# A graph network of four blocks on one core: the matrix that moves sums from rank to node order holds one over each node's count in place of one

## What is computed

```python
count = max(seg(ones), 1)                       # edges that end in a node, at least one
# block 0 (layer k = 0)
h = relu(h @ W_self.T + (seg(h[src]) / count) @ W_neigh.T + bias)
# block 1 (layer k = 1): product over edges of h[src] * edge_attr * filter(edge_weight), then softplus(agg @ W3 + b3)
# block 2 (layers k = 2, 3, 4), relu after the first two
h = (seg(h[src]) / count) @ W_agg[i] + h @ W_root[i] + b[i]
# block 3 (layers k = 5, 6, 7): attention with self loops, leaky relu, batch norm
h = leaky_relu(seg(ex * (h @ W)[src]) / denom + self_term + bias)
```

## Time and profile before

| | before |
|---|---|
| median of 3 runs | 8981.9 us (8965.29 to 8985.5) |
| profiled execution, its own time | 8979.64 us |
| profiled execution, span on the core | 8977.9 us |
| instructions | 96878 |
| busy: POOL, DVE, PE, ACT | 6350.5, 5163.1, 4441.1, 1376.7 us |
| TensorE clock granted, mean | 0.638 |

### The profile page before, as it was taken

The page is one execution under the profiler, slowest core; times in us unless marked ns, Lnnn a source line. Parts: engine busy times, 40 slices in busy tenths (PEclk is TensorE's granted clock), DMA queues, the critical chain, the costliest instruction groups (busy, mean ns, idle before and its releaser), DMA issues.

```text
span 8977.9 us, 96878 instructions
## 1 busy us (share of the span) xinstructions
PE 4441.1 (49%) x25313; PEld 3544.6 (39%) x25313; DVE 5163.1 (58%) x15662; ACT 1376.7 (15%) x2233; POOL 6350.5 (71%) x6609
## 2 busy tenths in 40 slices
PE   4655566665433344333533348354276452673532
PEld 3444433333433344333433345254253442543532
DVE  6786577776433343333433348686378773596844
ACT  6666634333100000000100010000010000100000
POOL 5777477776677767777677757777767777677774
PEclk7777777776655566565665555576555665656755
DMA  6555467775221121112211212332123331223311
GB/s 177 156 155 157 135 193 203 200 198 149 69 52 52 52 59 52 53 52 53 59 52 52 52 54 77 112 117 73 38 69 112 118 88 41 71 89 111 112 52 31
DMA packets 598961, 852.69 MB, mean 95 GB/s; under 512 B 130268, under 2 KB 404941, under 8 KB 597456
## 3 DMA queue, kind: packets, MB, share of 16 engines
q0 software_dynamic: 211168, 413.92, 17.8%
q1 hardware_dynamic: 372748, 381.31, 13.9%
q10 hardware_dynamic: 14688, 53.48, 1.5%
HBM read 652.71 MB, written 195.51 MB: 94 GB/s over the span
## 4 chain that ended last, share of the span: by engine, by line
POOL 69%; issue 24%; DVE 3%; PE 2%; DMA 1%; ACT 0%; POOLq 0%; ACTq 0%; DVEq 0%
POOL rows L821 41%; POOL rows L851 24%; POOL nd L834 2%; POOL at_first L827 2%; DMA rows<-table,src_t 1%; PE PS L1161 0%; POOL acc L868 0%; DVE H L1859 0%; DVE H L1858 0%; DVE H L2014 0%; DVE H L2013 0%; DVE H L2012 0%; DVE moments L1597 0%; PE PS L1169 0%; PE PS L1133 0%
## 5 line engine op out<-in xcount | busy, mean ns | idle before, releaser
L821 POOL DMA_INDIRECT rows<-table,src_t x3910 | 3724.7, 953 | 1491.2 <-issue 1263.9
L1667 DVE TENSOR_TENSOR acc<-acc,PS 128x128 f32 x5474 | 1552.7, 284 | 2956.5 <-PE PS L1244 1729.4
L851 POOL DMA_INDIRECT rows<-table,src_t x2346 | 2283.1, 973 | 923.2 <-issue 750.1
L1244 PE MATMUL PS<-onehot,rows 128*128 128x128 f32 x6256 | 1413.1, 417 | 2241.1 <-DMA rows<-table,src_t 2241.1
L1244 PEld LDWEIGHTS PS<-onehot,rows 128*128 128x128 f32 x6256 | 1305.5, 318 | 2404.4 <-DMA rows<-table,src_t 2403.6
L1280 PE MATMUL PS<-onehot,rows 128*128 128x128 f32 x3060 | 678.9, 411 | 1196.5 <-DMA rows<-table,src_t 1134.0
L1280 PEld LDWEIGHTS PS<-onehot,rows 128*128 128x128 f32 x3060 | 627.7, 313 | 1241.5 <-DMA rows<-table,src_t 1183.8
L1751 DVE TENSOR_SCALAR onehot<-PS,loc_t,shared 128x128 f32<-128x128 f32 x2346 | 940.4, 402 | 0.5
L924 ACT ACTIVATE rows<-acc 128x128 f32 x343 | 77.9, 297 | 2641.8 <-DVE acc L1667 2638.2
L1353 PEld LDWEIGHTS PS<-als_bf,onehot 128*128 128x128 bf16 x7056 | 308.3, 119 | 427.3 <-DVE onehot L1934 269.6
L1643 DVE TENSOR_TENSOR onehot<-PS,loc_t 128x1024 f32<-128x1024 f32 x392 | 476.7, 1217 | 0.2
(11 more groups left out here) (320 smaller groups left out, 5744.0 us busy)
## 6 DMA issues: line engine op xcount, KB each, us to landing
rows<-table,src_t POOLq DMA_INDIRECT x6256, 2.9
staged<-rows ACTq DMA_DIRECT2D x102, 512.0 KB
H<-staged SPq DMA_DIRECT2D x102, 512.0 KB
soft_rows<-shared SPq DMA_DIRECT2D x196, 256.0 KB
H<-soft_rows SPq DMA_DIRECT2D x98, 512.0 KB, 3.9
prod_rows<-onehot SPq DMA_DIRECT2D x98, 512.0 KB, 5.0
shared<-in_edge_weight SPq DMA_DIRECT2D x195, 256.0 KB, 3.5
G<-in_edge_attr SPq DMA_DIRECT2D x97, 512.0 KB, 6.2
```

Of the source, the lines that this page charges most:

```text
L821: pool.indirect_dma_start(rows[:, h * HT + j, :], None, table[k % 2], at(src_t[:, t:t + 1]))\
L851: pool.indirect_dma_start(rows[:, g % 2 * HT + j, :], None, table[k % 2], at(src_t[:, t:t + 1]))\
L1244: last = mm(window_at(k, c, j), rows[:, r, :], onehot[:, r, :], start=True, stop=True)
L1667: tt(at, at, window_at(k, c, j), ALU.add).then_inc(added[h], 1 if j < n - 1 else HT - n + 1)
```

## The change

The matrix holds `1 / count` of the node where it held a one. For that `make_perms` gets a second scalar and a second operation. In `mean_layer` the multiplication by `rcount` is gone, and the addition of `T` reads PSUM and gives the signal `nodes_used`. The attention layers use the same matrix but want no division by the count, so `self_weights` multiplies `rden_n` by the count once in each of them. For that `count` itself is now kept at one or more.

```diff
-                step(ts(rcount[:], count[:], 1.0, None, ALU.max))
-                step(recip(rcount[:], rcount[:]))
+                step(ts(count[:], count[:], 1.0, None, ALU.max))
+                step(recip(rcount[:], count[:]))
 
             def make_perms(m):
                 wait(v, perm_turned, m)
                 for j in range(min(PERM_BLOCKS, NT - m * PERM_BLOCKS)):
                     b = m * PERM_BLOCKS + j
-                    last = ts(perm_in[:, j * D:(j + 1) * D], iota_ps, plocal[:, b:b + 1], None, ALU.is_equal)
+                    last = ts(perm_in[:, j * D:(j + 1) * D], iota_ps, plocal[:, b:b + 1], rcount[:, b:b + 1],
+                              ALU.is_equal, ALU.mult)
                 last.then_inc(perm_made, 1)
...
                     v.wait_ge(nodes_ready, turn[k] * NCH + c + 1)
-                    step(tt(g, as_tiles(by_node(c)), per_node(rcount, c), ALU.mult), nodes_used)
-                    step(tt(g, g, t, ALU.add))
+                    step(tt(g, as_tiles(by_node(c)), t, ALU.add), nodes_used)
...
                 step(recip(rden_n, rden_n))
                 step(tt(exs_n, exs_n, rden_n, ALU.mult))
+                step(tt(rden_n, rden_n, count[:], ALU.mult))
                 step(tt(T3, T3, exs_n.unsqueeze(2).broadcast_to([P, NT, D]), ALU.mult))
```

## The result

The changed kernel takes 8950.3 us (median of 10 runs, 8935.3 to 8965.9). The kernel before, run beside it, takes 8968.7 us (median of 10, 8965.3 to 8985.5). The ratio is 0.9976 with a 95% interval of 0.9967 to 0.9985: about 21.5 us (0.24%) less, in an interval of 13.5 to 29.6 us. Forecast were 16.3 us less, 8965.6 us, and a result just within 0.2%. The time is inside the range of 8948 to 8982, but the gain is five microseconds larger than forecast and lies just beyond 0.2%. The two times themselves must not be compared: the forecast was counted from 8981.9 us, the median of three runs, and ten runs of the kernel before give 13.2 us less than that. Nor do the times alone exclude a gain of 16.3 us, which lies in their interval; the stretches of the profiles do.

What follows compares the result with a forecast made beforehand. It took POOL's gathers to set the pace within passes, with DVE mattering only where POOL waits. 3.1 + 3.1 + 5.4 + 5.4 - 0.7 = 16.3 us off the median 8981.9 gave 8965.6 us, range 8948 to 8982.

Steps and rivals of the forecast that it cites:

- Where the gain comes from: Removing the instruction pays only in four stretches, after the passes of layers 0, 2, 3 and 4, where POOL waits.
- Layers 2 and 3, 3.1 us each: After these layers' passes PE becomes the bound in place of DVE, so each stretch gains 3.1 us of 9.0 removed.
- Layers 0 and 4, 5.4 us each: After these layers' passes the removed multiplication stands eight times on the chain, so each stretch gains 5.4 us.
- both rings: Layer 4's two interleaved cycles through DVE, ACT and PE, two chunks per turn: each turn falls from 10.30 to 9.58 us.
- The clock rival: PE's clock rises in layer 4, about 9 us more, again if layer 0 follows: 8957 or 8948 us; chance 0.14.
- the sign of being wrong: Wrong if any stretch's granted clock changes level, L1859 takes other than 0.69 us, or the edge passes change length.
- The wait that moves in the rings: In layers 0 and 4 ACT or PE replaces DVE, so only stretch ends gain: 9.1 us, time 8973; chance 0.10.
- Slower, by PE at the lower clock in layers 2 and 3,: PE falls to its lower clock there, 27 us more per layer, time 9027 us; chance 0.05.
- The attention layers, -0.7 us: The new multiplication in self_weights delays the two large instructions and POOL by 0.24 us per layer, 0.7 us lost in three.
- the bound on the other side: In the attention layers one more gather might slip ahead of DVE's large instruction, gaining up to 1 us per layer.
- The matrix, nothing: L1745 takes 402 instead of 342 ns, 49 times, 2.9 us of DVE time hidden under waits for ACT: nothing lost.

Runs made afterwards that it cites:

- gat_late: The changed kernel with the attention layers' multiplication by count moved behind the two large instructions on T; ratio 0.9988 to the kernel before.
- after_again: The changed kernel run again without any edit, on another chip than the first; ratio 0.9986 to the kernel before.
- the busy pair: The two kernels before_busy and after_busy, both with idle PE matmuls in layers 0 and 4; ratios 0.9992 and 0.9984 to the kernel before.
- before_again: The kernel before run again without any edit, on another chip than the first; ratio 1.0001 to the kernel before.
- costs_only: The changed kernel with a multiplication by ones put back in all four mean layers, leaving only the added work; ratio 1.0004 to the kernel before.
- before_busy: The kernel before plus six unused PE matmuls after each chunk's block of L1169 in layers 0 and 4; ratio 0.9992 to the kernel before.
- after_busy: The changed kernel plus six unused PE matmuls after each chunk's block of L1169 in layers 0 and 4; ratio 0.9984 to the kernel before.
- after_order: The changed kernel with ACT copying the windows of chunk c + 2 right after the product of chunk c; ratio 0.9971 to the kernel before.

## Why the prediction was right, and where it was wrong

**Where the gain comes from** held. The four stretches in which POOL waits for the table are where the time went; the executions with and without the instruction differ there by 8.4, 2.3, 2.5 and 8.1 us (layers 0, 2, 3, 4; means over the table's rows up to gat_late, without the two busy ones, of 67.6 and 59.2, 30.3 and 28.0, 30.7 and 28.2, 67.5 and 59.5). That is 21.3 us, against a gain of 21.5 us by the times on the first chip, and 15.6 us with an interval of 5.6 to 25.6 in after_again.

**Layers 2 and 3, 3.1 us each:** the mechanism held to 0.01 us. DVE waits for PE at each chunk, the chunks come every 1.786 us, and DVE's part is 3.1 us shorter. The term was a little too large, 2.3 to 2.5 us measured, since I took the gain at DVE's last relu for that at the first gather. In the profiles of the first chip that last piece takes 2.22 us (3286.17 to 3288.39), 0.3 us more than before. That the stores come closer together now is my reading; no run tested it.

**Layers 0 and 4, 5.4 us each:** this is the step that failed. The prediction wrote "So both rings go to 10.30 - 0.72 = 9.58 us". The count of instructions in it was right within 0.7 us, as the busy pair shows. What failed was that PE's part of the turn, 3.89 us, was carried over at its length from before. In the kernel before, the block that decides ran at or near the lower level in nearly all of its turns. With 0.72 us less on DVE the old pattern (pauses of 0.9 and 1.8 us, or of 0.3 and 4) no longer holds, the pauses in the layer 4 shown above are 0.9 to 2.7 us without a fixed order, and in part of the turns the block that decides runs at the higher level, 1.16 us and not 2.08. All executions show it: in the four with the instruction and the four without it (no idle work, old order on ACT), I took the distance from each chunk's first read on DVE to that of the next but one, from chunk 1 to chunk 10 of layers 0 and 4, 64 distances of each kind. The mean goes from 10.05 to 8.59 us, 1.46 us less, of which the instruction is 0.73 and the level the other half. Without the instruction 12 of the 64 are 9.57 us, as forecast, and 21 are 7.84 to 7.92 us, the length at the higher level; the rest lie between.

**The clock rival** was thus right in its mechanism. It had 0.14, and the sign of being wrong that the prediction named, a granted clock that changes level, came for layer 4 (0.55 to 0.79). That its figure for both layers together, 8948 us, is 2 us from the measured 8950 is luck: it stands for a gain of 34 us, and 21.5 were measured; what is missing is made up by the 13 us by which the kernel before came out below 8981.9. Its 9 us per layer are too much, since the block that decides is fast in part of the turns only; even with the clock held at 0.94 the stretches of the kernel before get only 6.5 to 7 us shorter. Against it I had held that PE's share in layer 4 only goes from 75% to 81%. That was an argument from a mean, and before_again shows what a mean is worth: 0.75 of the clock in place of 0.55 and the same 68 us, since the faster half of the blocks lay off the path. What mattered was which of the two blocks in a turn is slow. The Trainium skill (TensorE: Matmul & The Clock Gate, section What's actually happening) gives the direction, a clock at half until activity releases it; the idle matmuls agree, with 0.94 where the same stretch had 0.75 and 0.55. It is a direction only: in the changed kernel one block came at 2.08 us after a pause of 0.92 and another at 1.16 after 2.65, so the pause just before a block doesn't settle its level.

**The wait that moves in the rings** is refuted: the turn is shorter by the instruction at either level. **Slower, by PE at the lower clock in layers 2 and 3,** is refuted: the granted clock there went from 0.98 to 1.00 in both. Its sum, 9027 us, was 6 us too high: 2.1 us per chunk are counted from PE's 1.79 us, so all 16.3 us of the forecast come off and not 10.1. Nothing else hangs on it.

**The attention layers, -0.7 us:** neither confirmed nor refuted, since the times and the passes differ by more than that between executions. In two of three layers a gather slipped through ahead of the block, the bound on the other side that the prediction named. That the new instruction itself would hold POOL, by the Trainium skill (SBUF — State Buffer, section Who interferes with whom), isn't seen: the one gather with which it overlaps for its length keeps 0.95 us. No gather starts well within it, though, so these executions hardly test it. And where a gather came first, DVE's large instruction took its 6.69 and 6.72 us all the same: in these executions only the gather was held, never DVE.

**The matrix, nothing:** L1745 takes the forecast 402 ns, and costs_only shows no difference within its interval.

**Left open.** What settles the level of a single block of PE, and so why the fast ones fell on the path more often after the change: the runs show that they did, in four executions each of layers 0 and 4, not how the chip chose. Also the passes over the edges, which took up to 1.7 us each longer in the profiled execution of the changed kernel than in that of before, 8.0 us in all. That lengthening of the passes was a sign of being wrong by the prediction's own words. On the other chips there is no such pattern: the passes of layers 2 to 4 differ by 0.3 us or less in two and by 1.2 in the third between before_again and after_again, while that of layer 1 took 1239.5 and 1264.6 us there, 1252.4 in before_busy and 1245.2 in after_busy. Differences of this kind come without the change too, and I take them for differences between executions; no run settles it.

## What to carry to other kernels

Where engines take turns in a ring with slack on all of them, don't carry PE's time over from the old profile: work out the turn at both of its lengths, since the removed instruction also changes PE's pauses, and let the range reach to the faster one. Look at which blocks on PE the next engine waits for, and at their durations one by one; the mean granted clock of the stretch can move by 0.2 without a change in its length. And when a ring is coupled by the order of one engine, try the order first: once DVE was the bound, the same removal was worth 8.8 and 7.0 of its own 9 us.

## What the runs showed that I had not expected

The same kernel before took 8.97 ms on the first chip and 11.07 to 11.15 ms on three others. It is not the gather instruction: its median is 945 ns on the first and 946 in before_again. It is what POOL waits for in between; from before_again (waiting line, releaser, us in total, times, longest):

```profile
POOL rows L851 <- PE PS L1280: 1070.8, 19, 344.9
...
POOL rows L821 <- remote: 550.6, 154, 4.7
POOL rows L851 <- remote: 296.9, 111, 7.2
...
POOL rows L821 <- DVE G L1782: 243.2, 41, 12.0
```

The changed kernel on the first chip has 18.2 us of the first kind and none of the others. The pass of layer 5 takes 1578 us there and 1144 on the first chip, that of layer 2 1117 and 987. In the kernel before the four stretches of this study have the same length on both within a microsecond, which is why they could be compared across chips. What holds up the gathers there no run here tells.

Six matmuls that nobody reads, added to each chunk, made a stretch 6.5 to 7 us shorter, because the path ran through PE at half its clock. The same six on top of after_order changed it by +0.8 and -1.7 us. In these runs idle work on PE paid only where PE's slow block was what the next engine waited for.
